# A routed feed-forward layer on one core: gathers limited to two under way, and the sums placed by the group steps

## The chip, the core and the metric

One Trainium2 chip, one core of it. The metric is the device time of one execution in microseconds (us). The kernel before took 1848.07 us (median of 3 runs, 1846.26 to 1850.08).

## The reference, cut to what matters

A transformer block over 16 sequences of 512 tokens, 128 channels: causal attention with 16 heads, then a feed-forward layer in which a router picks 8 of 160 experts for each token, with a shared expert beside them.

```python
x = x + ga * attention(layernorm(x) * (1 + ca) + sa)       # 16 sequences, 512 tokens, 128 channels
h = layernorm(x) * (1 + cb) + sb
probs = sigmoid(h @ router_w.T + expert_bias)               # 160 experts
top_w, top_idx = top_k(probs, 8)
top_w = 2.5 * top_w / sum(top_w)
routed[t] = sum over the 8 experts e of top_w[t, e] * (silu(h[t] @ w_gate[e].T) @ w_down[e].T)
shared = silu(h @ w_gate_shared.T) @ w_down_shared.T
x = x + gb * (routed + shared)
```

## The kernel before, in words

The program has two stages. The attention stage runs 16 turns, one per sequence. In it the first 14 sequences (`PAGED`) are routed: each token's row is copied by GpSimd's indirect DMAs (scatters, line 786) into pages in DRAM, a page holding 128 rows of one expert. The last two sequences (`FULL`) are not routed by pages.

The expert stage takes the pages in 152 groups of four. Step G of `b_step` does three things on TensorE: the down product of group G-2 (line 1562), the gate product of group G-1 (1546), and the transposes of group G (1525). ScalarE does the silu (1554) and, with VectorE for the first 50 groups, the copies (1576, 1573, 1536, 1533). `y_store` (1513, issued by ScalarE) writes a group's results to `results` in DRAM, in step G+3; it goes through a ring of four buffers, each with its own semaphore `s_ys`, and a copy into a buffer waits for the store that left it. SyncE loads weights (1499, four transfers a group) and page rows (1506), up to eight groups ahead, and it works through its list strictly in order.

Between the group steps stand three other kinds of work, in the order of the list `order`:

- *Shared steps* (lines 1281 to 1313), 16 of them between the group steps 34 and 60: the shared expert, whose products wait for VectorE (`scale`, 1297) and whose next product waits for VectorE's `add` (1313).
- *Dense units* (`full_unit`), 160 of them: the last two sequences go through all 160 experts, two experts a unit. TensorE does 1674 and 1679, ScalarE 1686, VectorE 1692, and TensorE 1698 one unit later. They begin at group step 63 (`OPEN`), 139 of them stand between the group steps, the rest behind the last one. `full_end` closes a sequence (1730 adds the result).
- *Sums* (`combine`), 56 of them, one for each tile T of 128 tokens: VectorE multiplies the eight gathered rows of each token by their weights (1625), adds them up (1627), multiplies by the gate (1629) and adds the result to x (1631). Sum T stands at group step 63 + 2T; what is left when the groups end is mixed with the left units, one sum for every five.

The rows of a sum come from `gathers` on GpSimd (1613): for each tile eight indirect DMAs, each of which reads one result row of 512 B for each of 128 tokens, 448 in all. The four tiles of a sequence may be gathered when all groups up to group 48 + 8n are stored (`s_ys`), and a tile's buffer is one of seven, so gathers of tile T wait for the sum of tile T-7 (`sum_d`); the first seven wait for the shared expert's products (`s_shu`), because the buffers lie over its input.

Engines work through their own instructions strictly in order, so a VectorE that waits for a gather also holds the multiply of every dense unit and every shared step that stands behind it.

Of the kernel before, what the change touches and what calls it, by code (L numbers as in the profile page):

```python
# [25 lines left out]
NB, S, D = 16, 512, 128  # L26
NT = S // P
H, HD = 16, 8
NE, TOPK, INTER = 160, 8, 64
GRP = 4  # L30
PAGED = 14
# [3 lines left out]
NGRP = NPAGE // GRP  # L35
# [16 lines left out]
TILES = 7  # L52
# [54 lines left out]
def build(nc, x, wts, brow, wexp, wpack, wds, const, constb, restb, constd, out):  # L107
    with ExitStack() as ctx:
# [3 lines left out]
        def sem(name):  # L112
            return ctx.enter_context(nc.semaphore(name))
# [233 lines left out]
        def xtile(n, t):  # L347
            return xr[:, bass.ds(n * NT + t, 1), :].rearrange("p o d -> p (o d)")
# [877 lines left out]
        s_shu, s_sha, s_shw, s_shd, s_shx = (sem(n) for n in ("s_shu", "s_sha", "s_shw", "s_shd", "s_shx"))  # L1226
# [5 lines left out]
        def gb(n):  # L1232
            return gb_half[n // 8][:, n % 8, :]
# [226 lines left out]
        def b_rows(d, G):  # L1460
            return d[bass.ds(G * GRP * P, GRP * P), :].rearrange("(p q) d -> p (q d)", q=GRP)
# [47 lines left out]
        def y_store(e, G):  # L1509

            e.wait_ge(s_YD, G + 1)
            e.wait_ge(s_YA, G + 1)
            e.dma_start(b_rows(results, G), y_sb[:, G % 4, :, :].rearrange("p j d -> p (j d)")).then_inc(s_ys[G % 4], 16)

        def b_step(G):

            pe, dve, act = [], [], []
# [67 lines left out]
            if G < NGRP:  # L1585
                pe.append(tr)
                (dve if G < SWITCH else act).append(xt)
            if 0 <= G - 3 < NGRP:
                act.append(lambda e: y_store(e, G - 3))
            return {name: (lambda e, fs=fs: [f(e) for f in fs])  # L1590
                    for name, fs in (("pe", pe), ("dve", dve), ("act", act)) if fs}


        s_gt = [sem(f"s_gt{i}") for i in range(TILES)]
        s_o = sem("s_o")
        sum_d = Events(sem("sum_d"), ["mul", "sum", "gate", "fin"])

        def ready(n):
            return NE // GRP + SPAN // GRP * (n + 1)

        def gathers(e, n):

            if n == 0:
                e.wait_ge(s_pos, 5)
            for g in range(4):
                e.wait_ge(s_ys[g], 16 * (ready(n) // 4))
            for t in range(NT):
                i, T = (n * NT + t) % TILES, n * NT + t
                if T < TILES:
                    e.wait_ge(s_shu, T + 1)  # L1610
                sum_d.wait(e, "sum", T - TILES)
                for k in range(TOPK):
                    e.indirect_dma_start(  # L1613
                        out=y8[:, i, k, :], out_offset=None, in_=results[0:ready(n) * GRP * P, :],
                        in_offset=bass.IndirectOffsetOnAxis(ap=pos_all[:, n, t * TOPK + k:t * TOPK + k + 1], axis=0),
                    ).then_inc(s_gt[i], 16)

        def combine(e, T):

            n, t, i = T // NT, T % NT, T % TILES  # L1620
            weights = wts_all[:, bass.ds(n, 1), t * TOPK:(t + 1) * TOPK].rearrange("p o (k c) -> p (o k) c", c=1)
            e.wait_ge(s_gt[i], 16 * TOPK * (T // TILES + 1))
            if T == 0:
                e.wait_ge(s_shx, NB)
            sum_d.done(e.tensor_tensor(y8[:, i, :, :], y8[:, i, :, :], weights.broadcast_to([P, TOPK, D]), ALU.mult), "mul")  # L1625
            sum_d.wait(e, "mul", T)
            sum_d.done(e.tensor_reduce(o_sb[:, T % 2, :], y8[:, i, :, :].rearrange("p k d -> p d k"), AX.X, ALU.add), "sum")  # L1627
            sum_d.wait(e, "sum", T)
            sum_d.done(e.tensor_tensor(o_sb[:, T % 2, :], o_sb[:, T % 2, :], gb(n), ALU.mult), "gate")  # L1629
            sum_d.wait(e, "gate", T)  # L1630
            sum_d.done(e.tensor_tensor(xtile(n, t), xtile(n, t), o_sb[:, T % 2, :], ALU.add), "fin")  # L1631
# [123 lines left out]
        OPEN, LASTG = SPREAD + 31, NGRP + 2  # L1755
        units = FULL * PAIRS

        def place_of(u):

            return OPEN + u * (LASTG - OPEN) // (units - LEFT) if u < units - LEFT else LASTG + 1  # L1760

        def sum_at(T):

            return OPEN + 2 * T

        order = []
        u = T = 0
        for G in range(NGRP + 3):
            order.append(("group", G))
            while u < units and place_of(u) <= G:  # L1770
                order.append(("unit", u))
                u += 1
            while T < PAGED * NT and sum_at(T) <= G:
                order.append(("sum", T))
                T += 1
        while u <= units or T < PAGED * NT:
            for _ in range(5):
                if u <= units:
                    order.append(("unit", u))
                    u += 1  # L1780
            if T < PAGED * NT:
                order.append(("sum", T))
                T += 1
        at = {step: k for k, step in enumerate(order)}

        def sp_order():

            due = []
# [43 lines left out]
        def tail():  # L1832
            return merge((routing(NB - 1), 0.0, 0.62, 0.6), ([b_step(G) for G in range(FIRST)], 0.02, 1.0, 0.0))
# [77 lines left out]
```

## Time and profile before

| | |
|---|---|
| median of the runs | 1848.07 us |
| span of the profiled execution (the page gives no other time of it) | 2225.1 us |
| TensorE matmul busy | 1632.8 us, 73% |
| VectorE busy | 1242.1 us, 56% |
| ScalarE busy | 828.9 us, 37% |
| GpSimd busy | 1007.3 us, 45% |
| DMA, mean | 166 GB/s |

The profile is of one execution, and its span is 377 us above the median of the runs, 20% of it. The page gives the span and no time around it. Busy time counts instructions only; the wait of one engine for another is in the views of waits and of the timeline. Times in the rows are us from the start of the span.

### The profile page before, as it was taken

How to read it: one execution, taken by the hardware profiler on the slowest of the kernel's cores; microseconds unless marked ns; L12 is line 12 of the kernel's file. 1: busy time of each engine (PE TensorE's matmuls, PEld its weight loads, DVE VectorE, ACT ScalarE, POOL GpSimd, SP SyncE). 2: the span in 40 equal slices, each digit the busy share in tenths (PEclk: the TensorE clock that was granted, in tenths of full speed). 3: DMA queues.
4: the chain of work that ended last, by engine and by line, in shares of the span. 5: the costliest groups of instructions: out<-in, count | busy, mean ns of one | idle time of the engine just before them, and what ended most of it. 6: DMA issues, size and time to landing. Idle time of an engine off the chain costs nothing. (4 is left out here: it accounts for less than half of the span.)

```text
span 2225.1 us, 33972 instructions
## 1 busy us (share of the span) xinstructions
PE 1632.8 (73%) x10822; PEld 771.5 (35%) x10822; DVE 1242.1 (56%) x4230; ACT 828.9 (37%) x1717; POOL 1007.3 (45%) x1054
## 2 busy tenths in 40 slices
PE   5568888788877787888875793467877777766684
PEld 2123333333333333333332562333433333333331
DVE  4757778777787678777653561033433433333347
ACT  1145444444444445444443431233333323322231
POOL 2011465565655555555553005445554555545553
PEclk9978888778888788878777897788989988878897
DMA  4774555455554554455334796656756656656432
GB/s 149 234 248 132 157 159 155 140 147 162 160 151 144 142 155 147 142 143 163 85 99 123 247 339 199 187 159 177 215 172 192 198 174 178 193 175 197 142 109 56
DMA packets 264985, 369.71 MB, mean 166 GB/s; under 512 B 41207, under 2 KB 141704, under 8 KB 264680
## 3 DMA queue, kind: packets, MB, share of 16 engines
q1 hardware_dynamic: 214248, 268.91, 41.9%
q0 software_dynamic: 28672, 58.78, 9.0%
q10 hardware_dynamic: 21888, 39.86, 4.8%
q8 instruction: 88, 1.44, 0.3%
q14 instruction: 89, 0.73, 0.1%
HBM read 219.79 MB, written 147.60 MB: 165 GB/s over the span
## 5 line engine op out<-in xcount | busy, mean ns | idle before, releaser
L1613 POOL DMA_INDIRECT vh<-results,pos_all x448 | 439.0, 980 | 537.6 <-DVE oT L1627 173.4
L786 POOL DMA_INDIRECT pages<-h,pos_s x448 | 434.8, 971 | 280.7 <-issue 110.9
L571 DVE CUSTOM_DVE_ANT_0 shelf<-bank,cb_all 128x512 bf16<-128x512 f32 (+3 forms) x1024 | 444.7, 485 | 187.9 <-PE bank L561 127.7
L675 ACT ACTIVATE prob<-bank 128x512 f32<-128x512 f32 x640 | 350.1, 600 | 428.8 <-PE bank L660 250.7
L1692 DVE TENSOR_TENSOR work<-work,bank 128x512 f32<-128x512 f32 x160 | 109.9, 687 | 486.9 <-ACT work L1686 314.7
L561 PE MATMUL bank<-km,qm 64*128 64x512 bf16 (+3 forms) x1024 | 213.7, 354 | 125.3 <-DVE rmax L571 87.5
L711 PE MATMUL bank<-prob,v_ext 128*32 128x512 f32 (+3 forms) x2048 | 238.1, 538 | 7.7 <-DVE onorm L737 4.0
L648 PE MATMUL bank<-qe,ke 64*128 64x512 bf16 (+3 forms) x1024 | 176.6, 342 | 64.4 <-issue 34.9
L1576 ACT ACTIVATE v_ext<-bank 128x256 f32<-128x256 f32 x254 | 86.5, 384 | 301.6 <-remote 132.9
L1562 PE MATMUL bank<-prob,ke 64*128 64x128 f32 x1216 | 117.3, 315 | 75.3 <-ACT ke L1554 42.5
L561 PEld LDWEIGHTS bank<-km,qm 64*128 64x128 bf16 x1024 | 52.8, 98 | 316.5 <-issue 188.9
L1686 ACT ACTIVATE work<-bank 128x512 f32<-128x512 f32 x160 | 96.0, 600 | 162.7 <-PE bank L1674 94.7
L1674 PE MATMUL bank<-vh,on_att 128*128 128x512 f32 x160 | 95.7, 684 | 72.9 <-ACT work L1686 57.5
L1562 PEld LDWEIGHTS bank<-prob,ke 64*128 64x128 f32 x1216 | 87.8, 203 | 172.7 <-issue 112.2
L1546 PE MATMUL bank<-qe,prob 128*64 128x128 f32 x1216 | 108.3, 302 | 32.5 <-issue 25.9
L648 PEld LDWEIGHTS bank<-qe,ke 64*128 64x128 bf16 x1024 | 52.1, 100 | 201.7 <-issue 146.9
L1525 PE MATMUL bank<-c_all,prob 128*128 128x128 f32 x608 | 107.8, 302 | 12.2 <-issue 10.4
L660 PE MATMUL bank<-cb_all 64*128 64x128 bf16 (+1 forms) x1280 | 114.6, 227 | 0.0
L1627 DVE TENSOR_REDUCE oT<-vh 128x128 f32<-128x1024 f32 x56 | 106.7, 1905 | 1.9
L1554 ACT ACTIVATE ke<-bank 128x256 f32<-128x256 f32 x152 | 58.6, 386 | 126.0 <-remote 86.3
L478 POOL TENSOR_TENSOR work<-work,shelf 128x512 f32<-128x512 f32 x32 | 36.9, 1153 | 129.2 <-ACT shelf L472 128.7
L1698 PE MATMUL bank<-work,on_att 128*128 128x512 f32 x160 | 89.6, 643 | 0.0
(209 smaller groups left out, 2401.8 us busy)
## 6 DMA issues: line engine op xcount, KB each, us to landing
prob<-wexp SPq DMA_DIRECT2D x448, 96.0 KB
pages<-free_rows SPq DMA_DIRECT2D x38, 1024.0 KB
prob<-pages SPq DMA_DIRECT2D x152, 256.0 KB
results<-v_ext ACTq DMA_DIRECT2D x152, 256.0 KB
qm<-q_stacks SPq DMA_DIRECT2D x64, 256.0 KB
km<-k_stacks SPq DMA_DIRECT2D x64, 256.0 KB
qe<-q_stacks SPq DMA_DIRECT2D x64, 256.0 KB
ke<-k_stacks SPq DMA_DIRECT2D x64, 256.0 KB
```

The source lines that it names most:

```text
L561: last = e.matmul(MX[g % 2][:, c0:c0 + (i + 1) * P], qm[rows_, c % 2, h, i * P:(i + 1) * P], km[rows_, c % 2, h, 0:(i + 1) * P], start=Tru ...
L571: last = e.tensor_tensor_reduce(out=masked[:, g % 2, c0:c0 + (i + 1) * P], in0=MX[g % 2][:, c0:c0 + (i + 1) * P], in1=mask_w[:, S - (i + 1 ...
L648: e.matmul(ST[g % 3][:, c0:c0 + S - j * P], ke[rows_, c % 2, h, j * P:(j + 1) * P], qe[rows_, c % 2, h, j * P:S], start=(k == 0), stop=Tru ...
L660: return e.matmul(out_, pick[rows_, :], over, start=False, stop=True, skip_group_check=True)
L675: e.activation(prob[:, slot, :], ST[g % 3][:, :], ACT.Exp, scale=SCALE).then_inc(s_exa, 1)
L711: last = e.matmul(PV[32 * g:32 * g + 32, j * P:S], v_ext[:, j, 4 * c + g, :], prob[:, (c % 2) * UNITS + u, c0:c0 + S - j * P], start=(j == ...
L786: e.indirect_dma_start(out=pages, in_=h2[:, t, :], in_offset=None, out_offset=bass.IndirectOffsetOnAxis(ap=pos_s[:, t * TOPK + k:t * TOPK ...
L1525: last = e.transpose(TX[G % 2][:, :].rearrange("d (p q) -> d q p", q=GRP)[:, q, :], x_in[G % DEEP][:, q, :], ident)
L1546: last = e.matmul(GT[half:half + 64, (j // 2) * P:(j // 2 + 1) * P], w_gate(G, j), x_T[G % 2][:, j * P:(j + 1) * P], start=True, stop=True)
L1562: last = e.matmul(YP[j % 2][:, (j // 2) * D:(j // 2 + 1) * D], h_g[G % 2][half:half + 64, (j // 2) * P:(j // 2 + 1) * P], w_down(G, j), st ...
L1613: e.indirect_dma_start(out=y8[:, i, k, :], out_offset=None, in_=results[0:ready(n) * GRP * P, :], in_offset=bass.IndirectOffsetOnAxis(ap=p ...
L1692: e.tensor_tensor(f_hw[u % 2], f_h[u % 2], FC[:, :], ALU.mult).then_inc(s_dm, 1)
```

## The change

Four things change. A gather waits until the gather two before it has landed: each tile's semaphore becomes a pair, one for even and one for odd gathers, and `landed` waits for the right one. `y_store` moves one group step forward, from step G+3 to G+2. Sum T moves from group step 63 + 2T to 54 + 2T, so that 51 instead of 46 sums stand between the group steps. Behind the last group eight units instead of five stand ahead of sum 52, the first of the last sequence. The wait for the shared expert's adds is spread: a sequence's first sum waits for the adds of its own pair of sequences, not sum 0 for all of them.

```diff
--- before.py
+++ after.py
@@ -1585,18 +1585,24 @@
             if G < NGRP:
                 pe.append(tr)
                 (dve if G < SWITCH else act).append(xt)
-            if 0 <= G - 3 < NGRP:
-                act.append(lambda e: y_store(e, G - 3))
+            if 0 <= G - 2 < NGRP:
+                act.append(lambda e: y_store(e, G - 2))
             return {name: (lambda e, fs=fs: [f(e) for f in fs])
                     for name, fs in (("pe", pe), ("dve", dve), ("act", act)) if fs}
 
 
-        s_gt = [sem(f"s_gt{i}") for i in range(TILES)]
+        s_gt = [[sem(f"s_gt{i}_{par}") for par in range(2)] for i in range(TILES)]
         s_o = sem("s_o")
         sum_d = Events(sem("sum_d"), ["mul", "sum", "gate", "fin"])
 
         def ready(n):
             return NE // GRP + SPAN // GRP * (n + 1)
+
+        def landed(e, q):
+
+            if q >= 0:
+                T, k = divmod(q, TOPK)
+                e.wait_ge(s_gt[T % TILES][k % 2], 16 * (TOPK // 2 * (T // TILES) + k // 2 + 1))
 
         def gathers(e, n):
 
@@ -1610,18 +1616,20 @@
                     e.wait_ge(s_shu, T + 1)
                 sum_d.wait(e, "sum", T - TILES)
                 for k in range(TOPK):
+                    landed(e, T * TOPK + k - 2)
                     e.indirect_dma_start(
                         out=y8[:, i, k, :], out_offset=None, in_=results[0:ready(n) * GRP * P, :],
                         in_offset=bass.IndirectOffsetOnAxis(ap=pos_all[:, n, t * TOPK + k:t * TOPK + k + 1], axis=0),
-                    ).then_inc(s_gt[i], 16)
+                    ).then_inc(s_gt[i][k % 2], 16)
 
         def combine(e, T):
 
             n, t, i = T // NT, T % NT, T % TILES
             weights = wts_all[:, bass.ds(n, 1), t * TOPK:(t + 1) * TOPK].rearrange("p o (k c) -> p (o k) c", c=1)
-            e.wait_ge(s_gt[i], 16 * TOPK * (T // TILES + 1))
-            if T == 0:
-                e.wait_ge(s_shx, NB)
+            for par in range(2):
+                e.wait_ge(s_gt[i][par], 16 * TOPK // 2 * (T // TILES + 1))
+            if t == 0:
+                e.wait_ge(s_shx, n // 2 * 2 + 2)
             sum_d.done(e.tensor_tensor(y8[:, i, :, :], y8[:, i, :, :], weights.broadcast_to([P, TOPK, D]), ALU.mult), "mul")
             sum_d.wait(e, "mul", T)
             sum_d.done(e.tensor_reduce(o_sb[:, T % 2, :], y8[:, i, :, :].rearrange("p k d -> p d k"), AX.X, ALU.add), "sum")
@@ -1759,9 +1767,13 @@
 
             return OPEN + u * (LASTG - OPEN) // (units - LEFT) if u < units - LEFT else LASTG + 1
 
+        def fetch_at(T):
+
+            return 51 + 2 * T
+
         def sum_at(T):
 
-            return OPEN + 2 * T
+            return fetch_at(T) + 3
 
         order = []
         u = T = 0
@@ -1773,8 +1785,8 @@
             while T < PAGED * NT and sum_at(T) <= G:
                 order.append(("sum", T))
                 T += 1
-        while u <= units or T < PAGED * NT:
-            for _ in range(5):
+        while T < PAGED * NT or u <= units:
+            for _ in range(8 if T == PAGED * NT - NT else 5):
                 if u <= units:
                     order.append(("unit", u))
                     u += 1
@@ -1782,7 +1794,6 @@
                 order.append(("sum", T))
                 T += 1
         at = {step: k for k, step in enumerate(order)}
-
         def sp_order():
 
             due = []
```

The change on GpSimd, in the first tiles of the gathers (of before, then of the change; `s_gt1_0` and `s_gt1_1` are the pair of tile buffer 1):

```order
L1613 DMA vh<-results,pos_all 128x128 [waits sum_d]
L1613 DMA vh<-results,pos_all 128x128 x7
L1613 DMA vh<-results,pos_all 128x128 [waits s_ys3,s_ys2,sum_d,s_ys1,s_ys0]
L1613 DMA vh<-results,pos_all 128x128 x7
L1613 DMA vh<-results,pos_all 128x128 [waits sum_d]
L1613 DMA vh<-results,pos_all 128x128 x7
```

```order
L1620 DMA vh<-results,pos_all 128x128 [waits s_gt1_0]
L1620 DMA vh<-results,pos_all 128x128 [waits s_gt1_1]
L1620 DMA vh<-results,pos_all 128x128 [waits s_gt1_0,s_shu]
L1620 DMA vh<-results,pos_all 128x128 [waits s_gt1_1]
L1620 DMA vh<-results,pos_all 128x128 [waits s_gt2_0]
L1620 DMA vh<-results,pos_all 128x128 [waits s_gt2_1]
```

What stood as seven gathers in a row without a wait is now seven gathers that each wait for the last but one.

VectorE around the first sum (1297 and 1313 are the shared expert's scale and add, 1692 a dense unit's multiply; the sum's four operations are 1625 to 1631 before and 1633 to 1639 in the change). Before:

```order
L1297 TENSOR_TENSOR work<-wds_sb,km 64x128 [waits s_shd]
L1297 TENSOR_TENSOR work<-wds_sb,km 64x128
L1313 TENSOR_TENSOR xr<-xr,bank 128x512 [waits s_shd]
L1313 TENSOR_TENSOR xr<-xr,bank 128x512
L1692 TENSOR_TENSOR work<-work,bank 128x512 [waits s_dc,s_da] x2
L1625 TENSOR_TENSOR vh<-vh,wts_all 128x1024 [waits s_shx,s_gt0]
L1627 TENSOR_REDUCE oT<-vh 128x128 [waits sum_d]
L1629 TENSOR_TENSOR oT<-oT,qm 128x128 [waits sum_d]
```

In the change:

```order
L1633 TENSOR_TENSOR vh<-vh,wts_all 128x1024 [waits s_shx,s_gt0_1,s_gt0_0]
L1635 TENSOR_REDUCE oT<-vh 128x128 [waits sum_d]
L1637 TENSOR_TENSOR oT<-oT,qm 128x128 [waits sum_d]
L1639 TENSOR_TENSOR xr<-xr,oT 128x128 [waits sum_d]
L1297 TENSOR_TENSOR work<-wds_sb,km 64x128 [waits s_shd]
L1297 TENSOR_TENSOR work<-wds_sb,km 64x128
L1313 TENSOR_TENSOR xr<-xr,bank 128x512 [waits s_shd]
L1313 TENSOR_TENSOR xr<-xr,bank 128x512
L1633 TENSOR_TENSOR vh<-vh,wts_all 128x1024 [waits s_gt1_1,s_gt1_0]
L1635 TENSOR_REDUCE oT<-vh 128x128 [waits sum_d]
L1637 TENSOR_TENSOR oT<-oT,qm 128x128 [waits sum_d]
L1639 TENSOR_TENSOR xr<-xr,oT 128x128 [waits sum_d]
```

The first sums moved from behind all shared steps and two dense units to places between the shared steps.

VectorE at the end, where the last dense unit is followed by the add of its sequence (1730 before, 1738 in the change). Before, where the last row begins the first of six sums:

```order
L1692 TENSOR_TENSOR work<-work,bank 128x512 [waits s_dd,s_dc,s_da] x5
L1625 TENSOR_TENSOR vh<-vh,wts_all 128x1024 [waits s_gt0]
L1627 TENSOR_REDUCE oT<-vh 128x128 [waits sum_d]
L1629 TENSOR_TENSOR oT<-oT,km 128x128 [waits sum_d]
L1631 TENSOR_TENSOR xr<-xr,oT 128x128 [waits sum_d]
L1730 TENSOR_TENSOR xr<-xr,bank 128x512 [waits s_up]
L1625 TENSOR_TENSOR vh<-vh,wts_all 128x1024 [waits s_gt1]
```

In the change, where the last row begins the last sum:

```order
L1700 TENSOR_TENSOR work<-work,bank 128x512 [waits s_dd,s_dc,s_da] x2
L1738 TENSOR_TENSOR xr<-xr,bank 128x512 [waits s_up]
L1633 TENSOR_TENSOR vh<-vh,wts_all 128x1024 [waits s_gt5_1,s_gt5_0]
L1635 TENSOR_REDUCE oT<-vh 128x128 [waits sum_d]
L1637 TENSOR_TENSOR oT<-oT,km 128x128 [waits sum_d]
L1639 TENSOR_TENSOR xr<-xr,oT 128x128 [waits sum_d]
L1633 TENSOR_TENSOR vh<-vh,wts_all 128x1024 [waits s_gt6_1,s_gt6_0]
```

Before, six sums stood behind that add, now two.

## Rows read from the trace of the kernel before

**Rows 1.** First line of the page.

```profile
span 2225.1 us, 33972 instructions
```

**Rows 2.** Windows: stretch, its us, busy us per engine, granted clock, DMA share, GB/s.

```profile
1300.00:1346.00 46.00, 42.37 (x454) 29.56 (x452) 29.73 (x61) 16.81 (x41) 0.00 (x0) 1.00 0.96 310
1346.00:1448.00 102.00, 37.75 (x324) 24.79 (x323) 5.79 (x14) 21.80 (x53) 53.55 (x56) 0.68 0.59 179
1448.00:2145.00 697.00, 504.83 (x2478) 253.47 (x2478) 258.22 (x320) 218.21 (x498) 349.46 (x357) 0.85 0.60 178
2145.00:2225.00 80.00, 43.80 (x116) 17.96 (x113) 54.32 (x66) 13.88 (x24) 36.00 (x36) 0.83 0.27 77
```

**Rows 3.** Timeline 1340 to 1400: start us, length us, engine, line, operation.

```profile
1346.07 1.91 SPq L1499 DMA_DIRECT2D prob<-wexp  x4
1346.12 0.33 ACTq L1513 DMA_DIRECT2D results<-v_ext  x1
...
1350.14 1.02 POOL L1613 DMA_INDIRECT vh<-results,pos_all  x1 [130.26 <-PE bank L1281]
...
1377.13 13.30 SPq L1499 DMA_DIRECT2D prob<-wexp  x4
1377.17 0.37 PE L1525 MATMUL bank<-c_all,prob 128*128 128x128 f32 x1 [2.42 <-issue]
```

**Rows 4.** Timeline around 2120: group steps on PE with one and two units between.

```profile
2111.36 0.96 POOL L1613 DMA_INDIRECT vh<-results,pos_all  x1 [0.30 <-issue]
...
2120.31 0.71 PE L1562 MATMUL bank<-prob,ke 64*128 64x128 f32 x8
...
2124.07 0.71 PE L1562 MATMUL bank<-prob,ke 64*128 64x128 f32 x8
...
2130.01 0.71 PE L1562 MATMUL bank<-prob,ke 64*128 64x128 f32 x8
```

**Rows 5.** Windows behind the gather issued at 2111.36.

```profile
2113.00:2114.00 1.00, 0.00 (x0) 0.00 (x0) 0.00 (x0) 0.00 (x0) 0.00 (x0) 0.50 0.24 66
2114.00:2115.00 1.00, 0.00 (x0) 0.00 (x0) 0.00 (x0) 0.00 (x0) 0.00 (x0) 0.50 0.00 0
```

**Rows 6.** Timeline: last scatter, and the first load that waits for all scatters.

```profile
1192.58 0.95 POOL L786 DMA_INDIRECT pages<-h,pos_s  x1 [0.30 <-issue]
...
1196.22 1.74 SPq L1506 DMA_DIRECT2D prob<-pages  x4
```

**Rows 7.** Timeline of the end: sums of the last tiles.

```profile
2183.95 1.90 DVE L1627 TENSOR_REDUCE oT<-vh 128x128 f32<-128x1024 f32 x1
...
2186.12 0.95 POOL L1613 DMA_INDIRECT vh<-results,pos_all  x1 [1.38 <-DVE oT L1627]
...
2194.93 1.53 POOL L1613 DMA_INDIRECT vh<-results,pos_all  x1 [0.30 <-issue]
...
2198.72 1.22 DVE L1625 TENSOR_TENSOR vh<-vh,wts_all 128x1024 f32<-128x1024 f32 x1
...
2202.42 1.22 DVE L1625 TENSOR_TENSOR vh<-vh,wts_all 128x1024 f32<-128x1024 f32 x1
...
2220.67 0.29 DVE L1631 TENSOR_TENSOR xr<-xr,oT 128x128 f32<-128x128 f32 x1
```

**Rows 8.** Waits of the whole span: who waited for whom, us, times, longest.

```profile
POOL vh L1613 <- DVE oT L1627: 173.4, 27, 15.5
...
ACT v_ext L1576 <- DMA results<-v_ext: 7.7, 6, 1.7
```

**Rows 9.** Timeline, ACT: one such row opens each turn of the attention stage.

```profile
149.14 0.48 ACT L605 ACTIVATE rmax_T<-bank 64x384 bf16<-64x384 bf16 x1 [9.37 <-PE bank L599]
...
207.02 0.48 ACT L605 ACTIVATE rmax_T<-bank 64x384 bf16<-64x384 bf16 x1 [3.33 <-PE bank L599]
...
1116.13 0.48 ACT L605 ACTIVATE rmax_T<-bank 64x384 bf16<-64x384 bf16 x1 [1.62 <-PE bank L599]
```

**Rows 10.** Line 1562 from 1300 to 1346: count, ns, first and last start (8 a step).

```profile
L1562 PEld LDWEIGHTS bank<-prob,ke x136: 182/188/188, 1302.8 to 1344.5; 64*128 64x128 f32 x136
```

## The prediction

> **What bounds the kernel now.** I read the page's first line, then the windows by stage, then the timeline of GpSimd, VectorE and the DMA issues in the expert stage, then the waits, and last the end of the program. The change touches nothing ahead of group step 49, so all that counts lies behind 1346 us, where the last store that the first gathers need is issued [rows 3]. From there to the end of the span are 2225 - 1346 = 879 us.
>
> In that stretch no engine is full. Until 1346 the DMA share is 0.96 and a group step takes 46/17 = 2.7 us (136/8 = 17 steps [rows 10]; DMA sets their pace); then it falls to 0.60, and TensorE is busy for 505 of 697 us [rows 2]. The reason stands in the timeline: while gathers run in a string, everything is slow. Four weight loads that SyncE issues in 1.91 us at 1346 take 13.30 us at 1377, and single matmuls of one transpose, which wait for nothing in the profile, stand 2.42 us apart [rows 3]. The profiled execution is 377 us longer than the median, so hold-ups of this sort must be largely missing in the runs. How many of the 377 us fall behind 1346 sets how much room the gathers have in a run, so I bound it.
>
> *Lower end of the stage in a run.* GpSimd alone: a gather takes 0.96 us and 0.30 us of idle ahead of it, 1.26 us [rows 4]. The first starts 4 us behind 1346 [rows 3], 447 intervals follow, and from the start of the last one to the end are 2225.1 - 2194.9 = 30 us [rows 1, 7]: 4 + 447 x 1.26 + 30 = 597 us. TensorE gives less: a group with one unit takes 3.76 us, with two 5.94 us [rows 4], so 88 groups and 139 units are 88 x 3.76 + 51 x 2.18 = 442 us, 13 opening steps 35 us, the rest behind the groups 80 us [rows 2]: 557 us.
>
> *Upper end.* A turn of attention takes 57.9 us before the scatters begin and (1116.1 - 207.0)/13 = 69.9 us afterwards [rows 9]. Were all the 12 us hold-ups, that would be 156 us ahead of 1346, and 221 of the 377 us would be left for this stage: 879 - 221 = 658 us.
>
> I take the middle, S = 627 us. Gathers at 1.26 us need 447 x 1.26 = 563 us of it: GpSimd has little to spare in a run, though the profile shows it busy for only 349 of 697 us [rows 2], waiting 173 us for the sums that free its buffers [rows 8].
>
> **The change, part by part.**
>
> *The cap.* Each gather but the first two now starts when the last but one has landed. With L from a gather's start to its landing and 0.27 us from an event to GpSimd's next start (VectorE's sum ends at 2185.85, the gather starts at 2186.12 [rows 7]), the interval is the larger of 1.26 and (L + 0.27)/2. The trace shows no wait for a gather, so L is bounded. From below: behind the string that ends with the gather started at 2111.36 nothing else moves; its data move between 2113 and 2114, and nothing afterwards [rows 4, 5], so L is 1.7 to 2.6 us on idle DMA. From above: the last scatter, an indirect DMA of the same size, starts at 1192.58, and the load that waits for all of them goes out at 1196.22 [rows 6]: 3.64 us, which may hold other waits. In a run the gathers go beside loads at a share above 0.60, so the idle value is an end, not the middle. I take L = 2.6, the top of the nearest row: interval 1.435 us. The ends are 1.26 (L up to 2.25, the cap is free) and 1.955.
>
> The chain of gathers is then: first start 1.4 us behind 1346 (the store goes out one step, 2.7 us, earlier), 447 intervals, landing of the last 2.6, its sum 3.7 (from 2198.72 to 2202.42 [rows 7]), the last store and the end 4.1 (from 2220.96). Total 447 x interval + 11.8: 575 us at 1.26, 653 at 1.435, 886 at 1.955. It reaches S at 1.376 us. At my value it sets the end: 653 - 627 = +26 us. What hides the gathers today is that VectorE asks for them 14 steps behind their tile's earliest start; the sums now stand nine steps earlier, so a late gather stops VectorE, behind it the unit's multiply (1692), then TensorE's down product (1698), then the groups.
>
> *The sums' places.* Behind the last dense unit stand two sums instead of six: 4 x 3.7 = -15 us [rows 7]. This counts only where TensorE sets the end. At the front it costs: sum 4 (step 62) needs 40 gathers, so it ends at 1.4 + 39 x 1.26 + 2.3 + 3.7 = 57 us behind 1346 even with a free cap, and 63 at 1.435. The first unit stands at step 63, which TensorE reaches after 13 steps of 2.7 us, 35 us, or 46 us if the gathers take their share of the DMA. The opening hold is 11 to 28 us, and shared steps queue behind the sums too. Five sums less among the units save at most 2 us each, and I put them at nothing beside this.
>
> *The store a step earlier.* It removes waits for a result buffer, 7.7 us over 6 waits of ScalarE [rows 8], if the load DMA does not take their place at once: 0 to -8, I take -5. ScalarE issues the same 152 stores; each waits for copies that stand ahead of it on ScalarE.
>
> *The rest.* GpSimd gets 446 waits more, whose price is within the 0.27. The eight units ahead of sum 52 keep TensorE busy while 8 gathers land (7 x 1.435 + 2.6 = 13 us against 8 x 2.18 = 17), and SyncE's list is unchanged but for the output stores, which move with their sums; the sequence-12 store goes ahead of the last sums instead of coming last, up to -0.5 us. Both are inside the error.
>
> Sum for the path of TensorE, with a free cap: -15 - 5 + (11 to 22) = -9 to +2 us. For the path of the gathers: +26 us, in which those gains have no part. Against the profiled execution's own span the chain at 1.435 (653 us) is far below its 879 us and would not show; there I expect -10 to -30 us. The forecast is for runs: 1848 + 26 = **1874 us**.
>
> The Trainium skill, "DMA: Bandwidth & Descriptors", section "Anatomy of one DMA — SWDGE (gpsimd) path", fits 2.0 us plus bytes over 436 GB/s for such a DMA, which is an estimated 2.15 us for 64 KB. By that rule (2.15 + 0.27)/2 = 1.21 us, the cap would be free, and the time that of the first rival; the idle string at 2113 agrees, and no row here tests it beside loads. The same page, section "Latency and other measured facts", gives the memory's latency as 0.2 us on average and 2 us under high load; an estimate from it is near 4 us for L, above the scatter's 3.64, and then the chain would take over 886 us.
>
> **The rivals.**
>
> *The cap is free and front and end cancel.* Landings stay under 2.25 us, and TensorE sets the end: -9 to +2 us, 1839 to 1850, middle 1843. For it speaks the idle landing; against it that loads run beside nearly all gathers.
>
> *Shorter strings free the loads.* If hold-ups like that at 1377 are partly there in runs, pacing the gathers gives the loads back their place. The stage could fall to the chain's 575 us at most, -52; with half of it -26, on top of no hold at the front: 1800 to 1832, middle 1820. For it: loads go seven times slower inside a string. Against: before, too, only two or three gathers fit into L at 1.26 us, so the cap takes one of them away at most.
>
> *Slower by the opening alone.* The stage is near 658 us, so the chain at 1.435 (653) has just room, but TensorE waits at step 63: 63 - 35 = 28 us less 20 gives +8; with 46 steps' time -3. 1845 to 1856. It decides where S exceeds 653.
>
> *The cap bites hard.* With L towards the scatter's 3.64 the interval passes 1.56 us: 709 us, +82, and above: over 1935.
>
> *The change does not do what it says.* If landings are so quick that no gather waits, the cap is nothing; that is the first rival's time.
>
> **How the numbers follow.** Forecast 0.42, its own range 1856 to 1935 (interval 1.39 to 1.57); free cap 0.28, of which 0.08 within no change; shorter strings 0.16; opening alone 0.09, of which 0.04 within no change; cap bites hard 0.05. A measurement of this kernel can tell about 0.2%, 3.7 us, from no change. Faster 0.20 + 0.16 = 0.36; same 0.08 + 0.04 = 0.12; slower 0.42 + 0.05 + 0.05 = 0.52. The range 1822 to 1935 leaves out half of the shorter strings and the hard bite, with the edges of the forecast about 0.17.
>
> **What would show it.** In the profile of the changed kernel: gathers start 1.4 to 1.5 us apart inside a sequence, with idle that ends at a DMA landing; the first sums wait on VectorE for gathers; TensorE idles for 11 to 28 us between step 54 and 63; two sums behind the last unit. Intervals of 1.26 us would make the cap free and my forecast wrong, and so would sums that never wait for a gather in a run shorter than before. A stage in which single matmuls and loads inside a string are no longer held would speak for shorter strings.

## The result: 13% slower, with the gathers 1.88 us apart

| | median of the runs | range | runs |
|---|---|---|---|
| before | 1847.16 us | 1844.54 to 1850.08 | 4 |
| changed | 2091.73 us | 2081.87 to 2096.82 | 4 |

The ratio is 1.130, 95% interval 1.126 to 1.134. The forecast was 1874 us with a range up to 1935: the direction was right, the size a tenth of what came. The time is that of the rival that I had called "the cap bites hard", with a chance of 0.05.

From the page of the changed kernel, its first line, which answers to [rows 1], and the line of GpSimd's gathers (the last part of that line is the idle time ahead of them and what ended most of it):

```profile
span 2094.5 us, 34082 instructions
...
L1620 POOL DMA_INDIRECT vh<-results,pos_all x448 | 462.5, 1032 | 509.3 <-DMA vh<-results,pos_all 329.4
```

Gathers now wait 329 us for earlier gathers, where the trace of before showed no such wait. The same gathers in the view of their line (count, shortest, median and longest in ns, first and last start):

```profile
L1620 POOL DMA_INDIRECT vh<-results,pos_all x448: 949/953/1891, 1243.5 to 2084.6; - x150
```

447 intervals fill 2084.6 - 1243.5 = 841.1 us, so the mean interval is 1.882 us. Ahead of the first gather the program takes nearly as long as before (1235.7 us in the second profile of before, below), behind the last one 2094.5 - 2084.6 = 9.9 us. The chain of gathers is the whole stage. The waits of GpSimd, VectorE and ScalarE from 1240 us on (who waited for whom, us, times, longest) show who pays:

```profile
POOL vh L1620 <- DMA vh<-results,pos_all: 329.4, 339, 3.9
...
DVE vh L1633 <- DMA vh<-results,pos_all: 266.6, 49, 11.9
...
ACT v_ext L1576 <- PE bank L1562: 256.4, 93, 21.3
```

49 of 56 sums wait for their gathers. VectorE executes in the order written, so units and groups behind a sum wait too, and ScalarE waits for TensorE's groups. The timeline of GpSimd near the start of the stage (start, length, engine, operation, idle ahead of it and what ended it) shows the interval itself:

```profile
1283.42 0.95 POOL L1620 DMA_INDIRECT vh<-results,pos_all  x1 [3.89 <-DMA vh<-results,pos_all]
1284.68 0.95 POOL L1620 DMA_INDIRECT vh<-results,pos_all  x1 [0.30 <-issue]
1287.69 1.89 POOL L1620 DMA_INDIRECT vh<-results,pos_all  x1 [2.06 <-DMA vh<-results,pos_all]
1290.11 0.96 POOL L1620 DMA_INDIRECT vh<-results,pos_all  x1 [0.53 <-DMA vh<-results,pos_all]
1292.94 0.95 POOL L1620 DMA_INDIRECT vh<-results,pos_all  x1 [1.87 <-DMA vh<-results,pos_all]
1294.19 0.95 POOL L1620 DMA_INDIRECT vh<-results,pos_all  x1 [0.31 <-issue]
```

The wait is uneven: a late landing holds one gather for 2 to 4 us, and the next goes out 0.3 to 0.5 us behind its end. Between 1300 and 1990 us the view of DMA gives the median from issue to landing:

```profile
vh<-results,pos_all POOLq DMA_INDIRECT x364, 3.1
```

### The profile page after: what moved, and what is told of

It is laid out like the page before. It is cut to its first block, busy times and chain, and to the rows that moved or that the text cites. A ratio compares the mean times of both kernels' runs of the same rounds, so it can differ in the third digit from the quotient of the medians.

```text
span 2094.5 us, 34082 instructions
## 1 busy us (share of the span) xinstructions
PE 1595.0 (76%) x10822; PEld 763.4 (36%) x10822; DVE 1236.6 (59%) x4230; ACT 838.1 (40%) x1717; POOL 1031.9 (49%) x1054
## 4 chain that ended last, share of the span: by engine, by line
DMA 35%; DVE 25%; PE 22%; issue 9%; POOL 5%; SPq 1%; ACT 1%; POOLq 0%; ACTq 0%; DVEq 0%
DMA vh<-results,pos_all 33%; DVE shelf L571 12%; PE bank L711 4%; POOL vh L1620 3%; PE bank L561 3%; PE bank L918 2%; PE bank L444 2%; PE bank L648 1%; PE bank L1546 1%; POOL pages L786 1%; PE bank L1525 1%; PE bank L455 1%; PE bank L725 1%; PE bank L850 1%; DVE work L466 1%
## 5 line engine op out<-in xcount | busy, mean ns | idle before, releaser
L1620 POOL DMA_INDIRECT vh<-results,pos_all x448 | 462.5, 1032 | 509.3 <-DMA vh<-results,pos_all 329.4
L711 PE MATMUL bank<-prob,v_ext 128*32 128x512 f32 (+3 forms) x2048 | 233.9, 538 | 6.1 <-DVE onorm L737 4.3
L1633 DVE TENSOR_TENSOR vh<-vh,wts_all 128x1024 f32<-128x1024 f32 x56 | 68.6, 1224 | 281.1 <-DMA vh<-results,pos_all 266.6
L1687 PE MATMUL bank<-shelf,c_all 96*128 96x512 bf16 x160 | 71.1, 444 | 198.9 <-DVE work L1700 198.9
L648 PE MATMUL bank<-qe,ke 64*128 64x512 bf16 (+3 forms) x1024 | 153.8, 326 | 18.6 <-DMA ke<-k_stacks 9.3
L1687 PEld LDWEIGHTS bank<-shelf,c_all 96*128 96x128 bf16 x160 | 16.8, 105 | 272.9 <-DVE work L1700 243.5
L660 PE MATMUL bank<-cb_all 64*128 64x128 bf16 (+1 forms) x1280 | 101.7, 217 | 0.0
```

The costliest lines, as they stand in the source:

```text
L648: e.matmul(ST[g % 3][:, c0:c0 + S - j * P], ke[rows_, c % 2, h, j * P:(j + 1) * P], qe[rows_, c % 2, h, j * P:S], start=(k == 0), stop=Tru ...
L711: last = e.matmul(PV[32 * g:32 * g + 32, j * P:S], v_ext[:, j, 4 * c + g, :], prob[:, (c % 2) * UNITS + u, c0:c0 + S - j * P], start=(j == ...
L1620: e.indirect_dma_start(out=y8[:, i, k, :], out_offset=None, in_=results[0:ready(n) * GRP * P, :], in_offset=bass.IndirectOffsetOnAxis(ap=p ...
```

## The experiments

There were eleven experiments: ten edited kernels, and the kernel before profiled a second time. Each ratio is to runs of the kernel before on the same chip. The first four take the cap apart from the rest and change its depth.

**The cap alone.** The kernel before, with the semaphores and the wait of the change, and nothing else of it:

```diff
                 for k in range(TOPK):
+                    landed(e, T * TOPK + k - 2)
                     e.indirect_dma_start(
```

> The kernel before with one part of the change alone: before gather q, GpSimd waits until gather q-2 has landed; sums, units and stores stand where they stood. Theory A (the cap sets the end): from the start of the first gather, 447 intervals of about 1.88 us follow as in the changed kernel, so that the stage from the first gather takes about 850 us where it took about 608: 2070 to 2110 us, 225 to 265 us above before. Theory B (the new places of sums and units cost most of it, by the hold in the opening; the cap costs what was forecast, 1.435 us a gather): 1865 to 1885 us. Theory C (half and half: the cap alone lets the units run on and recovers in the tail): about 1960 to 1980 us.

2105.16 us (2094.74 to 2117.82), ratio 1.137 (1.130 to 1.143). The row of its gathers:

```profile
L1620 POOL DMA_INDIRECT vh<-results,pos_all x448: 949/953/1982, 1262.5 to 2105.0; - x150
```

(2105.0 - 1262.5)/447 = 1.885 us, as in the changed kernel. This is theory A, in full: the cap alone gives the loss.

**No cap.** The changed kernel without the wait:

```diff
                 for k in range(TOPK):
-                    landed(e, T * TOPK + k - 2)
                     e.indirect_dma_start(
```

> The changed kernel without its cap: the gathers wait only for their results and their buffers, as before; the sums' places, the longer end group and the store one step earlier stay. Theory A (the cap sets the end): within 1835 to 1870 us, near the kernel before, and the gathers again 1.26 to 1.28 us apart where they run without a hold. Theory B (places and opening hold cost it): 2040 to 2080 us. By the terms of the forecast without that of the cap (tail -15, store -5, opening up to +28): 1827 to 1875 us.

1847.54 us (10 runs), ratio 1.000 (0.997 to 1.003). The places of the sums, the longer end group and the earlier store together change nothing that can be measured; the cap is the whole loss. Its gathers, and its window of 1450 to 1550 us (stretch, its us, busy us of TensorE, weight load, VectorE, ScalarE, GpSimd, granted clock, DMA share, GB/s):

```profile
L1620 POOL DMA_INDIRECT vh<-results,pos_all x448: 951/955/1990, 1245.7 to 1840.8; - x150
```

```profile
1450.00:1550.00 100.00, 94.57 (x527) 49.92 (x526) 54.78 (x67) 47.20 (x106) 77.41 (x75) 0.97 0.81 253
```

The interval is (1840.8 - 1245.7)/447 = 1.331 us, and 595 of the 611 us behind the first gather's start are gathers one behind the other. So without a cap GpSimd's rate of issue already bounds the stage, with TensorE, busy for 94.57 of 100 us, close beside it.

**Depths of three and one.** Wait on gather q-3, with four semaphores to a buffer in place of two, or on q-1:

```diff
-                    landed(e, T * TOPK + k - 2)
+                    landed(e, T * TOPK + k - 3)      # or k - 1
```

> The changed kernel with the wait on gather q-3 in place of q-2, so that three gathers may be under way; nothing else changes. Theory A1 (the interval is the time from a gather's start to its release, about 3.76 us beside the loads, over the depth): 3.76 / 3 = 1.25 us, below the 1.26 us of an issue; the stalls above the mean still cost some, so 1.28 to 1.40 us and 1850 to 1905 us. Theory A2 (the wait itself costs, whatever the depth, say the 0.5 us seen before most gathers): 447 x (0.95 + 0.3 + 0.5) = 782 us after 1242, 2025 us or more. Theory A3 (more gathers under way only lengthen each one's landing in proportion, so that the interval stays near 1.88 us): about 2090 us.

> The changed kernel with the wait on gather q-1: one gather under way at a time. Theory A1 (the time from start to release stays about 3.76 us, since it comes from the loads beside it): interval 3.76 us, 447 x 3.76 = 1681 us, total about 2930 us. Theory A3 (a gather alone lands sooner because it shares with no other gather): release after 2.7 to 3.1 us, total 2450 to 2640 us. Both theories on the sums' places give no number of their own here; a total below 2300 us would contradict the reading that the release of a gather sets the interval.

Depth three: 1947.73 us, ratio 1.053 (1.047 to 1.058), gathers from 1246.8 to 1938.0, 1.546 us apart. Depth one: 2711.54 us, ratio 1.465 (1.458 to 1.473), from 1245.8 to 2705.7, 3.266 us apart. Both fall between my theories A1 and A3: A1 had a start-to-release time that doesn't depend on the depth, A3 one that grows in proportion. Depth one also thins out the traffic beside the gathers: between 1300 and 1990 us all DMA together moves 104 GB/s, where it moves 179 in the changed kernel. At depth one an undisturbed gather looks like this (its last two):

```profile
2702.90 0.95 POOL L1620 DMA_INDIRECT vh<-results,pos_all  x1 [1.76 <-DMA vh<-results,pos_all]
2705.69 0.95 POOL L1620 DMA_INDIRECT vh<-results,pos_all  x1 [1.84 <-DMA vh<-results,pos_all]
```

2.79 us from start to start, the landing and the wake-up of the next gather together. With the 0.27 us that I had for the wake-up, L is 2.52, inside the idle bounds of 1.7 to 2.6 [rows 5]. The changed kernel's last gathers, two under way at most, show the same:

```profile
2081.83 0.95 POOL L1620 DMA_INDIRECT vh<-results,pos_all  x1 [0.48 <-DMA vh<-results,pos_all]
2083.16 0.95 POOL L1620 DMA_INDIRECT vh<-results,pos_all  x1 [0.38 <-DMA vh<-results,pos_all]
2084.60 0.95 POOL L1620 DMA_INDIRECT vh<-results,pos_all  x1 [0.48 <-DMA vh<-results,pos_all]
```

From the first of these starts to the third, which waits for the first gather's landing, are 2.77 us, no more than the 2.79 with one under way; the interval is 1.39 us. The idle value was read rightly, and at the quiet end of the stage the sum of the prediction holds; the mistake was to use it beside loads.

**Depth four.** The same with q-4.

> The changed kernel with the wait on gather q-4: up to four under way. Start to release was 3.27 us at a depth of one, 3.77 of two, 4.64 of three (mean interval times depth), so each further gather under way adds 0.5 to 0.9 us. Going on so: 5.4 us / 4 = 1.35 us, about the 1.33 us without a cap: 1850 to 1875 us. If instead a wait costs even where its gather has landed (0.05 us or more of register and semaphore work on each of 448): 1875 to 1900 us. If start to release grows in proportion from here (interval stays 1.55): about 1945 us.

1881.08 us, ratio 1.019 (1.014 to 1.024), gathers from 1227.6 to 1854.9, 1.403 us apart. The time is that of the second theory, but not for its reason: GpSimd's waits from 1300 us to the end are

```profile
POOL vh L1620 <- issue: 101.9, 323, 2.4
POOL vh L1620 <- DMA vh<-results,pos_all: 47.1, 72, 2.1
```

Where the wait found its gather landed, the idle is 101.9/323 = 0.32 us, against 0.30 without a cap, so a wait by itself costs at most 0.02 us. The rest are 72 late landings, 47.1 - 72 x 0.3 = 25 us.

The depths side by side. The waits are those of GpSimd for a gather's landing, in the whole span. The median from issue to landing and the DMA rate are of 1300 to 1990 us for the depths one and two, of 1300 to 1850 for three, of 1300 to 1750 for four; the trace holds the landing of every gather at depth one, of fewer at each further depth, and of too few for a median at depth four.

| under way at most | interval | waits for a landing | issue to landing | GB/s | ratio |
|---|---|---|---|---|---|
| 1 | 3.266 us | 439 | 2.6 us | 104 | 1.465 |
| 2 | 1.882 | 339 | 3.1 | 179 | 1.130 |
| 3 | 1.546 | 137 | 3.7 | 220 | 1.053 |
| 4 | 1.403 | 85 | | 254 | 1.019 |
| no cap | 1.331 | 0 | | | 1.000 |

The interval times the depth (3.27, 3.76, 4.64 and 5.61 us) is near the time from start to release only where most gathers wait for a landing. At three and four most don't: GpSimd's own 1.26 us sets their distance, and three or four of these are already 3.78 and 5.04 us. So these products don't show how the landing grows with the depth. Landings do come later from row to row, but the DMA rate rises with them, and the depth series can't tell the two apart. What it does show is that a typical landing doesn't give the price: at depth three (3.7 + 0.27)/3 = 1.32 us, and 1.546 was measured. One late landing holds GpSimd, and the gathers behind it can't make that up, since they go out 1.26 us apart at best.

**Light loads.** The changed kernel with the loads beside the gathers cut down from group 64 on, so that it computes in part on weights and rows of earlier groups; the instructions and their waits stay:

```diff
+                        w = 16 if G >= 64 else WROW
-                        e.dma_start(w_in[G % DEEP][:, j, :], wexp[bass.ds(wrow[g * GRP + j], P), :]) \
+                        e.dma_start(w_in[G % DEEP][:, j, 0:w], wexp[bass.ds(wrow[g * GRP + j], P), 0:w]) \
...
+            w = 16 if G >= 64 else GRP * D
-            e.dma_start(x_flat[G % DEEP], b_rows(pages, G)) \
+            e.dma_start(x_flat[G % DEEP][:, 0:w], b_rows(pages, G)[:, 0:w]) \
```

> The changed kernel, cap of two kept, with the traffic beside the gathers cut: from group 64 on each load of an expert's weights brings 16 columns in place of the whole row (96 KB), and each load of a group's rows of pages 16 columns in place of the whole 256 KB. So part of the weights and rows are those of earlier groups; every instruction and every wait is still there. Theory L (a gather's landing is late because of the loads beside it, and this is what lifts the interval from the 1.54 us of the undisturbed string at the end to 1.88 us): interval 1.55 to 1.65 us, stage 447 x 1.6 + 12 = 727 us, total 1945 to 1985 us. Rival (the landing is late for a reason of its own, results' stores or GpSimd's own port): interval stays 1.8 to 1.9, total 2060 us or more.

2019.4 us, ratio 1.093 (1.088 to 1.098). The windows of 1300 to 1990 us, first the changed kernel, then this one:

```profile
1300.00:1990.00 690.00, 497.81 (x2418) 251.38 (x2417) 259.73 (x321) 219.40 (x486) 377.57 (x364) 0.83 0.59 179
```

```profile
1300.00:1990.00 690.00, 536.67 (x2582) 267.62 (x2583) 296.25 (x367) 236.41 (x517) 420.25 (x411) 0.88 0.42 114
```

Gathers stand from 1246.9 to 2007.7, 1.702 us apart; the median from issue to landing fell from 3.1 (the row above, 1300 to 1990) to 2.7 (1300 to 1900). The result lies between the theory and its rival: what was cut from these loads makes up 0.18 us of the interval. The cut takes bytes and not packets: 105228 packets in these 690 us, 69953 of them under 512 bytes, against 100892 and 15229 in the changed kernel. With two gathers under way and 114 GB/s in all, the median landing of 2.7 is close to the 2.6 with one and 104, so most of its rise goes with the loads, not with the second gather. In the changed kernel's end, where the page's last two slices move 91 and 72 GB/s, 12 intervals from 2030.15 to 2048.53 are 1.53 us each, and the last five, from 2077.67 on, 1.39. What lies between these and 1.70 (the stores of results, the dense weights, the many small packets) is not taken apart.

**The kernel before, profiled again.** No edit.

> The kernel before, unchanged, profiled a second time. The profile on which the forecast rests spans 2225 us, 377 above the runs of the same kernel. Theory D (that execution was disturbed, and its 879 us from the first gather to the end were no measure of the stage): span 1845 to 1865 us, first gather near 1246, 448 gathers 1.32 to 1.34 us apart, last gather near 1842, idle of 0.30 us before nearly all. Rival (profiling this kernel always costs that much): span about 2200 us again.

One run, 1843.82 us. The first line of its page and its gathers:

```profile
span 1841.8 us, 33972 instructions
...
L1613 POOL DMA_INDIRECT vh<-results,pos_all x448: 951/955/1997, 1235.7 to 1831.4; - x150
```

And its window of 1350 to 1750 us, then that of the changed kernel:

```profile
1350.00:1750.00 400.00, 381.82 (x2101) 197.06 (x2100) 226.01 (x282) 190.72 (x422) 309.11 (x299) 0.99 0.85 263
```

```profile
1350.00:1750.00 400.00, 297.28 (x1469) 150.15 (x1468) 149.91 (x186) 132.08 (x294) 217.06 (x210) 0.85 0.61 187
```

Theory D, with a span 3 us below its band. The profiled execution on which the forecast rests was disturbed, by what no run shows; of this kernel there are only these two profiles. Its store at 1346.12 [rows 3] stands at 1231.33 here, so of the 383 us between the two spans 115 lie ahead of it and 268 behind. In this execution TensorE is busy for 95% of these 400 us, and in its whole string of gathers GpSimd never idles for more than 0.32 us between two; the 0.60 DMA share and the idle TensorE of [rows 2] belong to that one execution. The cap brings just that picture back, 0.61 and 74%, for a reason of its own.

**The store a step earlier, alone.**

```diff
-            if 0 <= G - 3 < NGRP:
-                act.append(lambda e: y_store(e, G - 3))
+            if 0 <= G - 2 < NGRP:
+                act.append(lambda e: y_store(e, G - 2))
```

> The kernel before with the store of a group's results one step earlier, nothing else. Forecast term: -5 us (first gather one step earlier): 1842 to 1846 us. Rival (GpSimd's first gather waits for the last store of ten steps, and ScalarE reaches it no sooner): 1847 to 1853 us, no difference.

1855.24 us beside 1854.06, ratio 0.999 (0.996 to 1.002): no difference that can be told. The interval reaches from -8 to +4 us, so it doesn't exclude the forecast's -5.

**A faster version.** In the kernel without the cap 595 us are spent where 447 x 1.26 = 563 would do. The longer gathers all stand at one place: where VectorE multiplies (1524 to 1528 us of that kernel, VectorE's multiply and reduction and GpSimd's gathers):

```profile
1524.66 1.22 DVE L1633 TENSOR_TENSOR vh<-vh,wts_all 128x1024 f32<-128x1024 f32 x1
1524.72 1.99 POOL L1620 DMA_INDIRECT vh<-results,pos_all  x1 [0.30 <-issue]
1525.91 1.93 DVE L1635 TENSOR_REDUCE oT<-vh 128x128 f32<-128x1024 f32 x1
1527.01 0.96 POOL L1620 DMA_INDIRECT vh<-results,pos_all  x1 [0.30 <-issue]
```

The gather that starts 0.06 us behind the multiply takes 1.99 us, until 0.83 us behind the multiply's end; the one beside the reduction takes 0.96. The Trainium skill, "SBUF — State Buffer", section "Who interferes with whom", says that a VectorE instruction with two inputs in SBUF contends with a GpSimd instruction that reads SBUF; the trace agrees for this multiply and a gather, which reads its row numbers there. Two kernels, both on the kernel before: the multiply in four pieces, and as eight multiplies by a column of weights.

```diff
-            sum_d.done(e.tensor_tensor(y8[:, i, :, :], y8[:, i, :, :], weights.broadcast_to([P, TOPK, D]), ALU.mult), "mul")
+            for c in range(0, TOPK, 2):
+                part = e.tensor_tensor(y8[:, i, c:c + 2, :], y8[:, i, c:c + 2, :],
+                                       weights[:, c:c + 2, :].broadcast_to([P, 2, D]), ALU.mult)
+            sum_d.done(part, "mul")
# or
+            for c in range(TOPK):
+                part = e.tensor_scalar(y8[:, i, c, :], y8[:, i, c, :], weights[:, c, :], None, ALU.mult)
+            sum_d.done(part, "mul")
```

> The kernel before, with VectorE's multiply of a sum (128x1024, 1.225 us) written as four of 128x256 one behind the other. In the kernel without the cap 48 of 448 gathers took 1.1 to 2.0 us on GpSimd in place of 0.95, each begun while that multiply ran and each over 0.83 us after it ended; in all 34 us of the 595 between first and last gather. Theory P (the gather's start on GpSimd waits for the end of the VectorE instruction under way, and gets in between two): the wait falls from 0.55 us on average to at most 0.2, gain 54 x 0.35 = 19 us, if the stage is bound by GpSimd's issue: 1825 to 1838 us. Theory Q (the pieces follow so closely that GpSimd still waits for the last, and the four take 1.7 us): no gain or up to 10 us lost, 1848 to 1860 us. Theory R (TensorE, busy for 94% of that stretch, binds as well): 1840 to 1850 us whatever GpSimd gains.

> The kernel before, with the multiply of a sum written as eight multiplies of 128x128 by a column of weights (one tensor and a scalar per partition in place of two tensors), about 0.31 us each by rows of the same form, 2.5 us in place of 1.225. VectorE has the time (53% busy in this stretch). Theory P (GpSimd's start of a gather is held only by an instruction with two tensors read from SBUF): no gather is held, 48 x 0.6 = 29 us gone from GpSimd's chain of 595 us, less the 1.3 us by which each sum is longer at the end: 1820 to 1835 us. Rival (any VectorE instruction of this sort holds it as long as it runs, or TensorE binds): 1843 to 1860 us.

Four pieces: 1823.83 us, ratio 0.984 (0.980 to 0.988). Eight columns: 1830.52, ratio 0.990 (0.986 to 0.994). Their gathers, in this order:

```profile
L1613 POOL DMA_INDIRECT vh<-results,pos_all x448: 952/958/1175, 1247.5 to 1819.0; - x150
```

```profile
L1613 POOL DMA_INDIRECT vh<-results,pos_all x448: 951/955/1076, 1246.4 to 1812.5; - x150
```

No gather takes more than 1.18 or 1.08 us; the intervals are 1.279 and 1.266 us, 24 and 30 us less than the 596 of the kernel before. Theory P holds for both (the four pieces came 1 us below its band), and the 26 us between the medians of before and of the four pieces agree with the 24 of the chain. TensorE did not bind before that. The eight columns have the shorter chain of gathers and yet the longer median; the intervals of the two ratios overlap. The ends of the two profiled executions differ. VectorE with eight columns, the add that closes the last sequence and the first and last of six sums, then with four pieces, the last sum:

```profile
1797.96 0.68 DVE L1732 TENSOR_TENSOR xr<-xr,bank 128x512 f32<-128x512 f32 x1
1798.56 1.65 DVE L1626 TENSOR_SCALAR vh<-vh,wts_all 128x128 f32<-128x128 f32 x8
...
1819.26 1.65 DVE L1626 TENSOR_SCALAR vh<-vh,wts_all 128x128 f32<-128x128 f32 x8
```

```profile
1821.57 1.43 DVE L1626 TENSOR_TENSOR vh<-vh,wts_all 128x256 f32<-128x256 f32 x4 [6.21 <-DMA vh<-results,pos_all]
```

With the eight columns the six sums behind the last dense unit run without a pause, 4.1 us each where before took 3.7 [rows 7], and VectorE sets the end, 15.1 us behind the last gather's start; with the four pieces the last sum waits for its gathers, and the end comes 10.7 us behind. That places the 4 us in these two executions; whether it makes the medians differ is not shown.

**The same without the cap but with the rest of the change.**

> The changed kernel without its cap, with the multiply of a sum in four pieces: sums' places, end group and the earlier store added to the version that measured 0.984 of before. There the gathers took 571 us from first to last, where 447 x 1.26 = 563 is what GpSimd needs, so only what lies ahead of the first gather or behind the last can still change. Forecast terms tail -15 and store -5: 1805 to 1820 us if they are real beside that chain. Rival (the last gather and its sum set the end, the opening's first gather the start, and the places change neither): 1818 to 1830 us, the same as in the run with the four pieces alone.

1835.5 us, ratio 0.987 (0.982 to 0.992): above both bands, and on the rival's side in that the forecast's gains don't appear. The last gather starts at 1817.5, and the span ends at 1836.7, 19.2 us later, where the four pieces alone needed 1829.7 - 1819.0 = 10.7. The end of VectorE's timeline shows why:

```profile
1825.07 0.69 DVE L1740 TENSOR_TENSOR xr<-xr,bank 128x512 f32<-128x512 f32 x1 [3.92 <-PE bank L1735]
1825.68 1.42 DVE L1634 TENSOR_TENSOR vh<-vh,wts_all 128x256 f32<-128x256 f32 x4
...
1829.58 1.42 DVE L1634 TENSOR_TENSOR vh<-vh,wts_all 128x256 f32<-128x256 f32 x4
```

With more units at the end, the last two sums stand behind the last dense unit's output, not behind their gathers, which end sooner.

The lowest ratio is that of the kernel before with its multiply in four pieces: 1.6% below before, 12.8% below the changed one (1823.83/2091.73 = 0.872, of medians from different sets of runs). Its interval overlaps those of the other two versions with a rewritten multiply.

## Why the prediction was wrong, by its steps

*The interval of the cap, the step that failed.* I wrote the interval as (L + 0.27)/2 and took L = 2.6, "the top of the nearest row", which gave 1.435 us. It measured 1.882. 447 x 0.447 = 200 us, and the miss is 218; nearly all of the rest is the 17 us of S below. The form was right up to a point: the upper end, 1.955, held, and on quiet DMA, at the changed kernel's own end, the interval was 1.39 us, below my 1.435. But I had written in the same place that the idle value "is an end, not the middle", and then used it as the middle. What was missing is the loads: beside them the median landing is 3.1 us, and single ones are far later (idles of 1.9 to 3.9 us in the timeline above), which the gathers behind can't make up. That a second gather under way makes each later is not shown: from start to release are 2.77 us with two in the last string, 2.79 with one. With the scatter's 3.64 [rows 6] as the nearest row, the sum would have given 1.955 us and 886 us of stage, 1848 + 886 - 627 = 2107 us, 15 off. Part of that nearness is luck: with the measured stage of 610 us it would be 2124, 32 off.

*The stage in a run, S = 627 us.* Measured 1841.8 - 1231.3 = 610 us in the second profile, inside my 597 to 658, and my 627 is 17 above it. The lower end, from GpSimd alone, was the better one: gathers fill the stage in a run, at 1.333 us. My upper end put up to 156 us of hold-ups ahead of the stage; they were 115.

*Against the profiled execution.* I expected -10 to -30 us there. It was 2225.1 to 2094.5, -131, and the number means nothing, since 268 us of the old stage were the disturbance. It has the opposite sign of the loss in the runs.

*The opening.* Forecast 11 to 28 us of hold at step 63. Without the cap TensorE waits once, 13.4 us; with it the waits from 1255 to 1340 us are

```profile
PE bank L1687 <- DVE work L1700: 18.4, 1, 18.4
PE bank L1306 <- DVE work L1297: 17.8, 2, 10.2
PE bank L1682 <- DVE xr L1313: 8.5, 1, 8.5
```

44.7 us in all, which fits my own sum for the hold with 1.882 us in it, 1.4 + 39 x 1.882 + 2.3 + 3.7 - 35 = 46 us. Neither sets the end: the chain of gathers runs on through it.

*The tail, -15 us.* Wrong in sign where it can be seen. From the last gather's start to the end of the span it is 16.1 us without the cap against 10.4 in the second profile of before, and 19.2 against 10.7 with the multiply in pieces. Two sums instead of six stand behind the last unit, but that unit now comes later than the last gathers. Of single executions, so the 6 and 8.5 us are no more than the places of the rows show. The eight columns show where the term would count: there six sums behind the last unit do set the end. No run moved them away there.

*The store, -5 us.* Run alone it changed nothing that can be told, which doesn't exclude 5 us.

*The price of 446 waits.* "Within the 0.27": at most 0.02 us for a wait whose gather has landed, as said.

*The rivals.* "The cap is free" and "shorter strings free the loads" both fall with the depth series: every cap up to four costs. The second rested on the hold-ups of [rows 3]; in the second profile of before the DMA share beside unbroken gathers is 0.85 at 263 GB/s, and the cap took it down to 0.61, so there was nothing to free. "Slower by the opening alone" falls with the kernel without the cap. "The cap bites hard" had the right mechanism, place and sign, and 0.05 of the chances, though my own bounds put the interval between 1.26 and 1.955 us and this rival began at 1.56, more than half of that range.

## What to carry to other kernels

Where an engine issues a long string of transfers and its rate already fills the stage, a cap on those under way costs at least (start to release)/depth - interval for each of them, where that is above zero, and late single landings come on top. Read the release from a transfer that goes beside the same traffic, not from an idle one, and look at the late ones as well as the median. When a profiled execution is 20% longer than the runs, profile again before taking a busy share or a stage's length from it. And look at the single lengths of the instructions in the string: here the longer ones pointed at 24 us that one rewritten multiply gave back.

## What the runs showed of the hardware

- One execution of an unchanged kernel spanned 2225.1 us and another 1841.8; the longer one held single matmuls and loads within strings of gathers.
- From start to release an indirect gather of 128 rows of 512 bytes took 2.79 us alone and 2.77 us with a second one under way, at the quiet ends of the program. Beside this stage's traffic the mean was 3.27 us with one and 3.76 with two, and the median from issue to landing 2.6 us with one under way and 104 GB/s of all DMA together, 3.1 with two and 179, 3.7 with three and 220.
- Gathers on GpSimd without a wait between them started 1.26 us apart, 0.95 busy and 0.30 idle.
- A gather that starts during a VectorE multiply of two tensors ends 0.83 us behind that multiply's end, up to 1.99 us long in place of 0.95 (48 of 448 in the kernel without the cap were held so); beside a reduction one took 0.96, and where eight multiplies by a column took the multiply's place none took more than 1.08.
